# A decoder layer on one core: the order of small steps at the turn from one group to the next, and in group 0

## The reference, cut to what matters

```
x = layernorm(x + mixer_block(x))
xn = layer_norm(x);  cn = layer_norm(ctx)
q  = xn @ Wq  (16 heads of 64);   k, v = split(cn @ Wkv)
out = softmax(q k^T / 8 + mask) @ v @ Wout + (silu(gate) * val) @ W2      # val, gate = split(xn @ W1)
x = layernorm(x + out)
h = relu(x @ w1.T + b1);  out = quantise(quantise(h) @ quantise(w2).T + quantise(b2))
x = layernorm(x + out)
```

## Time and profile before

| | us |
|---|---|
| median of three runs | 1914.57 (1913.03 to 1915.65) |
| the profiled execution's own time | 1913.43 |
| its span, from first to last instruction | 1911.6 |
| start of the attention's first step (group 0) | 649.5 |
| start of the query block that ends group 0 | 769.8 |
| one group from there on | 154.7 |
| PE busy | 1800.1, 94% |
| DVE busy | 1285.3, 67% |
| ACT busy | 925.4, 48% |
| POOL busy | 418.2, 22% |

### The profile page before, as it was taken

How to read it: one execution, slowest core, us unless ns; L and a number is a source line. 1 busy time by engine, 2 the same in 40 slices (tenths; PEclk the granted TensorE clock), 3 DMA queues, 4 the chain that set the end, 5 groups by cost and what they waited for, 6 DMA issues and landing times.

```text
span 1911.6 us, 28245 instructions
## 1 busy us (share of the span) xinstructions
PE 1800.1 (94%) x9512; PEld 1056.6 (55%) x9512; DVE 1285.3 (67%) x3970; ACT 925.4 (48%) x2262; POOL 418.2 (22%) x569
## 2 busy tenths in 40 slices
PE   4389999999999998999999999999999999999997
PEld 2266676676677544454554554544545554555466
DVE  6578888888885578367567647647746656764743
ACT  3334634544541456445545545545645644554542
POOL 4748678677773001000000000000000000000000
PEclk8689999999999999999999999999999999999999
DMA  4000000000002324223222222223222222223200
GB/s 128 1 1 11 11 11 11 20 11 11 11 29 77 116 77 150 53 63 76 68 63 68 62 66 71 63 61 77 63 58 75 69 63 67 65 63 69 53 13 20
DMA packets 73007, 102.46 MB, mean 54 GB/s; under 512 B 10304, under 2 KB 67584, under 8 KB 71968
## 3 DMA queue, kind: packets, MB, share of 16 engines
q1 hardware_dynamic: 72400, 100.20, 19.6%
q10 hardware_dynamic: 464, 0.46, 0.1%
HBM read 93.25 MB, written 7.39 MB: 53 GB/s over the span
## 4 chain that ended last, share of the span: by engine, by line
PE 90%; DVE 6%; ACT 1%; issue 1%; DMA 1%; SPq 0%; DVEq 0%; ACTq 0%
PE ps L1483 20%; PE ps L1438 9%; PE ps L1445 9%; PE ps L1476 9%; PE ps L1461 8%; PE ps L293 7%; PE ps L430 6%; PE ps L412 4%; PE ps L376 4%; PE ps L392 3%; PE ps L1543 2%; PE ps L1583 1%; PE ps L1537 1%; PE ps L362 1%; PE ps L1549 1%
## 5 line engine op out<-in xcount | busy, mean ns | idle before, releaser
L1822 DVE CUSTOM_DVE_ANT_0 x_pr<-ps,x_mk 128x375 f32<-128x375 f32 x448 | 227.7, 546 | 310.3 <-issue 198.5
L1694 ACT ACTIVATE x_pT<-ps 125x384 f32<-125x384 f32 x448 | 195.4, 489 | 265.1 <-PE ps L1445 264.2
L1700 ACT ACTIVATE x_pr<-x_pr,x_mx 128x375 f32<-128x375 f32 x448 | 268.1, 607 | 36.8 <-DVE x_mx L1822 36.5
L1445 PEld LDWEIGHTS ps<-ident,x_pr 128*125 128x125 f32 x1344 | 163.8, 187 | 129.5 <-issue 89.9
L1438 PE MATMUL ps<-x_kT,x_qT 64*128 64x375 f32 x896 | 202.5, 527 | 23.7 <-DVE x_mx L1822 17.7
L1445 PE MATMUL ps<-ident,x_pr 128*125 128x128 f32 x1344 | 206.1, 289 | 0.1
L1483 PE MATMUL ps<-x_xn,x_w 128*128 128x448 f32 x512 | 203.8, 541 | 0.0
L1831 DVE TENSOR_SCALAR x_pr<-x_pr,x_rc 128x375 f32<-128x375 f32 x448 | 169.9, 422 | 8.0
L1461 PE MATMUL ps<-x_pT,x_va 125*64 125x512 f32 (+1 forms) x768 | 160.0, 552 | 0.6 <-ACT x_pT L1694 0.6
L293 PE MATMUL ps<-m_xa,w_in 128*128 128x448 f32 x352 | 145.7, 561 | 5.7 <-ACT m_xa L525 5.7
L1438 PEld LDWEIGHTS ps<-x_kT,x_qT 64*128 64x128 f32 x896 | 68.2, 184 | 144.0 <-issue 114.7
(11 more groups left out here) (198 smaller groups left out, 2910.0 us busy)
## 6 DMA issues: line engine op xcount, KB each, us to landing
x_mk<-in_mask SPq DMA_DIRECT2D x224, 187.5 KB, 2.4
x_cx<-in_context SPq DMA_DIRECT2D x32, 375.0 KB
x_cT<-in_context_turned SPq DMA_DIRECT2D x32, 375.0 KB, 3.2
x_rb<-context_roots SPq DMA_DIRECT2D x32, 187.5 KB, 5.2
x_mixed<-m_x SPq DMA_DIRECT2D x8, 448.0 KB, 3.4
X<-x_mixed SPq DMA_DIRECT2D x8, 448.0 KB, 4.0
m_X<-in_x SPq DMA_DIRECT2D x7, 448.0 KB, 4.0
out<-f_so SPq DMA_DIRECT2D x7, 448.0 KB, 3.4
```

The lines of the kernel that those rows point to most:

```text
L1445: last = pe.transpose(bank(2 + e)[0:JP, t * ROWS:(t + 1) * ROWS], pr[:, 2 * (p % SLOT) + e, t * JP:(t + 1) * JP], ident[:, :])
L1694: act.activation(pT[:, 2 * NV * (batch(p) % 2) + 2 * (p % NP % NV) + e, :, :].rearrange("p t s -> p (t s)"), bank(2 + e)[0:JP, 0:JT * ROWS ...
L1700: act.activation(pr[:, k, :], pr[:, k, :], ACT.Exp, scale=-1.0, bias=mx[:, k:k + 1], accum_out=sums[:, k:k + 1]).then_inc(h_e.sem, 1)
L1822: dve.tensor_tensor_reduce(pr[:, k + e, :], bank(e)[:, 0:J], mk[:, p % SLOT, :], -1.0, 3.0e38, ALU.add, ALU.min, mx[:, k + e:k + e + 1]).t ...
```

## The change

Five edits, all of order; the operations and their sizes stay the same.

1. TensorE, groups 1 to 7: in step 0 the `turn` of step 26 of the group before stands in front of the scores, not behind them.
2. TensorE, groups 1 to 7: parts 0 and 1 of the first half of `out` go from steps 1 and 2 to steps 0 and 1. Step 2 has no part any more.
3. VectorE, groups 1 to 7: the final norm's statistics go from step 25 to step 26, its root from 26 to 27; the application stays in 27, behind the root.
4. VectorE, group 0: root and application of the norm for the last but one mixer result go from steps 0 and 1 to before the first keys' piece, the first statistics of the next context from step 0 to between that piece and the values' piece, the casts from step 8 to step 5, and the application for the last result from step 11 to 12 (`MLP_NORM`).
5. SP, group 0: two actions hang on `MLP_NORM`. The store of the last mixer result goes from step 13 to 14, the four weight loads from step 15 to 16.

```diff
-RESULT, TOKENS, FINAL = (10, 11, 12), (20, 21, 22), (25, 26, 27)
+RESULT, TOKENS, FINAL = (10, 11, 12), (20, 21, 22), {STEPS - 2: (0,), STEPS - 1: (1, 2)}
...
-            at[4 * c + n + 1, "Y"].append(("out", c, n))
+            at[4 * c + n + (1 if c or n >= 2 else 0), "Y"].append(("out", c, n))
...
-MLP_DOWN, MLP_SUM, MLP_ROOT, MLP_NORM = (1, 2, 3, 4), (2, 4), 10, 11
+MLP_DOWN, MLP_SUM, MLP_ROOT, MLP_NORM = (1, 2, 3, 4), (2, 4), 10, 12
...
+                if p == 0 and not first:
+                    turn(*back(it, p, 2))
                 scores(it, p)
...
-                if p >= 2 or not first:
+                if p >= 2 or (p == 1 and not first):
                     turn(*back(it, p, 2))
...
-                if r in CONTEXT and not (last and b == GB - 1):
+                if r in CONTEXT and not (last and b == GB - 1) and not (first and p == 0):
...
-                if first and p == 0:
-                    roots_result(LAST - 1, 2)
-                if first and p == 1:
-                    normed_result(LAST - 1)
...
-                if first and p == 8:
+                if first and p == 5:
                     dve.wait_ge(l_down.sem, 2 * 16)
                     dve.tensor_copy(fw2q[:, :, :], fw2, saturate=False).then_inc(s_q.sem, 1)
...
-                if not first and p in FINAL:
-                    final_norm(it - 1, FINAL.index(p))
+                for stage in FINAL.get(p, ()) if not first else ():
+                    final_norm(it - 1, stage)
...
         context_norm(-1, 0, 2)
+        roots_result(LAST - 1, 2)
+        normed_result(LAST - 1)
         part(-1, ("kv", 0))
+        context_norm(0, 1, 0)
         part(-1, ("vback", 0))
```

## The result

| | before | after |
|---|---|---|
| median | 1914.20 (1913.03 to 1915.65, 4 runs) | 1897.31 (1896.17 to 1899.57, 4 runs) |
| the profiled execution's own time | 1913.43 | 1896.43 |
| its span | 1911.6 | 1894.6 |
| one middle group | 154.69 | 152.47 |

The ratio of the times is 0.991, with a 95% interval of 0.9894 to 0.9926: the changed kernel is faster, by 16.9 us between the medians. A second comparison, of four further runs of the changed kernel with seven of the one before, gave 1898.08 against 1914.73, ratio 0.9914 (0.9899 to 0.9929). The second set's median of 1898.08 lies 0.58 inside it. The direction was right, and so were the mechanisms at the turns; the size was too small.

A forecast was written before the change was run, and what follows sets the result against it. TensorE, busy 1800.1 of 1911.6 us, bounds the kernel; only its waits can be gained. 6.8 + 6.1 + 1.1 + 0.6 = 14.6 us off 1913.43 gives 1898.8, plus 1.14 to the median: 1900.0; range 1897.5 to 1905.0.

The forecast's parts named there:

- GpSimd's hold: Group 0, step 16: halving W2 holds VectorE's division, due at 729.7, to about 732.8, leaving 0.6 of 1.5 us.
- Final norm one step later: Before the scores of step 27: the whole wait goes, 5 x 1.08 + 1.44 = 6.8 us; moved stages cost nothing.
- Turn in front, and parts one step sooner: Steps 0 and 1 at group turns: waits of 0.68 and 0.33 go, 1.01 at six turns, 1.1 at turn 0/1.
- the 0.18 that the forecast kept: Turn 0/1, before the scores of step 0: the turn fills 0.76 of the 0.94 wait and 0.18 stays.
- Step 2 and the roots' slack (1.6 and 2.1 us): After each turn: step 2 without a part leaves 1.6 us slack, the context's roots through memory 2.1; cost 0.
- waits are renewed: Rival, 11%: at the turns the slack is too little and half of the 14 us comes back; 1907.0.
- the roots come late at each turn: Rival, 4%: the scaling in step 4 waits for roots, each of six turns loses 2.8 us more; slower, 1917.
- Group 0: First group: casts leaving VectorE's chain give 1.5 us before step 10's scores; 0.6 is left after GpSimd's hold.
- The cast's wait: Group 0, before the scores of step 10: casts leave VectorE's chain, the 1.60 us wait gives 1.5.
- The first rival: 20%: hold falls on steps 17 to 19, roots late, -1.3 for +0.6; wider gap before step 23 slows clock, 1.5; 1903.4.
- a held scaling of the context: Group 0: if POOL starts 3 us later, the context's scaling is held, about 2 us worse, sum 12.7 for 14.6.
- one us of noise: Allowance in the forecast's own range: 1898, from 1.5 for group 0 and one us of noise, to 1902.

The follow-up runs named there:

- the pieces: The changed kernel, but GpSimd halves W2 in 8 pieces of 128x256 in place of one operation of 128x2048; 1899.26 us in one run.
- taking away only the first: The changed kernel with the next token norm's three stages in group 0 moved from steps 20, 21, 22 to 3, 13, 16; 1897.32 us.
- taking away both: Changed kernel, group 0: token norm in steps 3, 13, 16; next context's statistics and root in 19, 20, their way through memory in 21, 22; 1892.92 us.

## Why the prediction was right and where it was too small

The path and the cover at the turns were right. The step that failed is the price of the terms: the sum of 14.6 us took each wait at its idle time and let GpSimd's hold take back most of group 0's gain, and the profiles show 16.0 from the first scores on. Of the missing 1.4, 0.92 lie in the six groups, 0.33 in group 0 and 0.2 at the end.

- **Final norm one step later.** Mechanism, place and cover as forecast; the term was mis-sized, 6.8 for a measured 7.3 (1.16 in place of 1.08 each, 1.50 in place of 1.44). What failed is reading the idle time as the price. Matmuls that follow each other overlap at their ends (scores last 0.90 us and the next matmul starts 0.83 behind their start), and scores that wait lose the overlap ahead of them.
- **Turn in front, and parts one step sooner.** Costed together, which was right: the two alone gave 0.00 and 0.40 in a middle group and 1.06 together. The sum of 1.01 took the two waits at their idle 0.68 and 0.33. From start to start they were 0.84 and 0.50, and 0.3 came back: a turn of 0.84 between queries and scores in place of the 0.76 reckoned, 3.21 in place of 3.10 for a part that follows scores, 0.85 in place of 0.75 for a turn ahead of scores. Two errors that nearly cancelled. So the two terms, 7.2 us in the sum, measured 7.6: 6.57 in the six groups and 1.05 at the last turn (210.33 against 211.38 us behind the last query block, in two executions without the slow clock). Turn 0/1 gave 1.31 in place of 1.1 (154.94 to 153.63), since the 0.18 that the forecast kept did not stay.
- **Step 2 and the roots' slack (1.6 and 2.1 us).** Right: no wait of TensorE in a middle group, at any of the turns. The rivals "waits are renewed" and "the roots come late at each turn" fall.
- **Group 0.** Forecast 0.6; the pair of profiles shows 0.93. Over more profiles, the query block came after 120.37 on average in six without edits 4 and 5 and after 119.26 in three with them (119.41, 119.23 and 119.13), a gain of 1.1. The cast's wait gave 1.44 as reckoned (1.5). The hold was priced too dear: the forecast let it take back 0.9, and up to the scores of step 23 it took back 0.25 in the changed kernel's first execution (100.02 in place of 101.21) and nothing in its second (99.76) and with edits 4 and 5 alone. In the first, GpSimd started 76.97 us after the first scores, where the forecast had 77.5, the division came free at 82.9 in place of 83.3, and the scaled context was made 1.19 sooner, not 0.6. What is left after step 23 is scatter of two kinds: a slow clock behind the 3.41 us wait that cost the changed kernel's profile 1.3 us more than that of before (106.75 against 106.62 at the scores of step 24, after 100.02 against 101.21 at those of step 23), and the roots' wait of 0.92 that it did not have. The first rival named this clock as a danger, but the gap before step 23 did not widen: 3.41 in both. In the profile of before the slow rows begin with `times_v` (3.65), in its second execution already with the scores (1.62), behind the same wait.
- **GpSimd's hold.** Its reading, from two rows of the mixer, was right. In the changed kernel gate, `value` and `highest` ran beside GpSimd at their usual length (0.54 at 728.06), the divisions were held. With one long operation of GpSimd the pair of divisions ended 0.5 us behind it in each of the executions looked at, whether it had taken 2.14, 2.64, 3.57 or 4.49 us. The Trainium skill ("SBUF — State Buffer", section "SBUF: two separate sides") calls it an exclusive lock for a whole instruction; the pieces, 1.02 in place of 2.64, agree. Its case against this change, a held scaling of the context, did not arise: GpSimd ended at 730.84, the scaling began at 734.32.
- **Profiled time and median.** The forecast carried 1.14 us from one profiled execution to the median and allowed "one us of noise". That was too little: the start of the attention alone scatters by 4.5 us between executions, the clock behind one wait near the end by 1.7, the roots' way by 1.5. Of the 17.0 us between the two profiles 0.99 are such scatter. With 1.16 and 1.06 for a turn the sum would have been 15.6 or so, 1899, and the same 2.5 us to the low side would have held the result. So the prices of the waits alone make the difference between outside and inside. That it lies outside by 0.19, and the second set of runs inside by 0.58, is chance: the two sets of the changed kernel differ by 0.8 us.

What stays open: why TensorE's clock falls behind the wait of 2.05 us in 8 of 14 executions and not in the others; the wait itself has the same length in all 14. The Trainium skill ("TensorE: Matmul & The Clock Gate", section "Part 1: The HAM clock gate") says that the chip's looks at the engine's activity run freely and don't start with the kernel, so that one kernel gets slow stretches of differing length from run to run. That would fit both this and the first 100 us; no run here shows the looks themselves.

## What to carry to other kernels

Price a wait by the distance from start to start against the same pair of instructions where nothing waits, not by the idle time alone; the difference was 0.06 to 0.17 us for each of twenty waits here. Two edits at one wait are to be costed as a pair: filling it can move it whole to the next instruction that the same chain bounds. And where a wait is long enough for the clock to fall, look for the work that makes it and for what is late next, both at once: taking away only the first gave no clear gain here, taking away both gave 4.9 to 5.2 us.

## What the runs showed that was not expected

- Fifty microseconds in which TensorE is starved (20 us busy of 50, granted 0.63 to 0.66) are where two executions of one program went apart; over all profiles the start of the attention differed by up to 4.5 us, and that difference stays to the end.
- The same wait of 2.05 us was followed by 2.4 GHz in 6 executions and by a slow stretch in 8, worth 1.5 to 1.7 us.
- The clock that fell behind the 3.41 us wait cost 2.95 us in the changed kernel, nearly as much again as the wait. From the scores of step 23 to the next took 5.4 to 6.8 us in the eleven executions with this wait and 3.77 where the clock stayed up, so it cost 1.6 to 3.0.
- When GpSimd's long operation begins scatters by 1.5 us between executions of kernels with the same loads (76.48 to 77.97 after the first scores), and the wait that its hold leaves before the scores of step 19 went from 0.36 to 1.54 us with it.
- Eight pieces of 128x256 took GpSimd 6.65 us where one operation of 128x2048 took 5.37, and held VectorE for 0.3 us in place of 1.9.
